# Reordering TensorE's sums in the closing normalisation of a graph-attention layer

## What is computed

```python
Q, K, V = x @ Wq, x @ Wk, x @ Wv
score = exp(clip(einsum(K[src], Q[dst]) * scale, -5, 5))
h_attn = segment_sum(V[src] * score, dst) / (segment_sum(score, dst) + 1e-6)
h = x + h_attn
mean = h.mean(axis=0); var = ((h - mean) ** 2).mean(axis=0)
y = (h - mean) * rsqrt(var + 1e-5) * bn_gamma + bn_beta      # over the nodes
z = x + y
out = (z - z.mean(-1)) / sqrt(z.var(-1) + 1e-5)              # over the features
```

## Time and profile before

| | us |
|---|---|
| median of 3 timed runs | 2000.03 (1999.54 to 2001.93) |
| the profiled execution's own time | 1993.93 |
| its span, first to last instruction | 1992.2 |
| stage A, VectorE's first instruction of `normalise` to its first subtraction | 1840.6 to 1889.7 |
| stage B, to VectorE's first `times_amp` | 1889.7 to 1927.4 |
| stage C, to the end | 1927.4 to 1992.2 |

### The profile page before, as it was taken

How to read it: one execution, slowest core, us unless ns; L and a number is a source line. 1 busy time by engine, 2 the same in 40 slices (tenths; PEclk the granted TensorE clock), 3 DMA queues, 4 the chain that set the end, 5 groups by cost and what they waited for, 6 DMA issues and landing times. The chain is left out here.

```text
span 1992.2 us, 42376 instructions
## 1 busy us (share of the span) xinstructions
PE 1905.1 (96%) x7908; PEld 1348.2 (68%) x8018; DVE 1725.7 (87%) x2477; ACT 1365.2 (69%) x4578; POOL 1362.4 (68%) x1698
## 2 busy tenths in 40 slices
PE   8999999996899999999999999999999999998788
PEld 4555555554677777777777777777777777776233
DVE  6679555555899999999999999999999999999788
ACT  0000000003899999999999999999999998998657
POOL 0103343345788888888888888888888887885776
PEclk9999999997999999999999999999999999999989
DMA  5537766768999999999999999999999999999307
GB/s 188 170 128 228 242 222 226 242 230 286 332 333 331 340 350 350 333 338 349 348 347 338 336 347 348 350 336 338 344 350 344 340 345 336 339 356 346 110 17 289
DMA packets 184221, 588.87 MB, mean 296 GB/s; under 512 B 28432, under 2 KB 30192, under 8 KB 184176
## 3 DMA queue, kind: packets, MB, share of 16 engines
q0 software_dynamic: 135904, 465.14, 64.6%
q1 hardware_dynamic: 44752, 121.39, 17.6%
q10 hardware_dynamic: 3520, 1.81, 0.3%
HBM read 535.01 MB, written 78.91 MB: 308 GB/s over the span
## 5 line engine op out<-in xcount | busy, mean ns | idle before, releaser
L656 POOL DMA_INDIRECT kv<-kv_d,idx x880 | 909.3, 1033 | 235.6 <-issue 207.5
L742 ACT ACTIVATE kv<-kv 128x64 f32<-128x64 f32 x3520 | 889.3, 335 | 14.3
L830 PE MATMUL acc<-kv,mm_sb 128*128 128x260 f32 x3520 | 844.0, 383 | 6.2 <-ACT kv L742 0.6
L830 PEld LDWEIGHTS acc<-kv,mm_sb 128*128 128x128 f32 x3520 | 667.8, 190 | 104.3 <-issue 1.0
L809 PE MATMUL q_ps<-q_tile,mm_sb 128*128 x1760 | 539.9, 429 | 29.5 <-issue 7.2
L694 DVE TENSOR_TENSOR kv<-q_ps,kv 128x1024 f32<-128x1024 f32 x440 | 537.9, 1222 | 28.8 <-issue 14.6
L701 DVE TENSOR_REDUCE raw<-kv 128x16 f32<-128x1024 f32 x440 | 532.2, 1210 | 0.0
L809 PEld LDWEIGHTS q_ps<-q_tile,mm_sb 128*128 128x128 f32 x1760 | 316.7, 189 | 167.6 <-issue 124.3
L616 DVE TENSOR_TENSOR kv<-kv 128x384 f32<-128x384 f32 x440 | 249.9, 568 | 16.7 <-ACT kv L756 16.6
L752 ACT ACTIVATE mm_sb<-mm_ps,less 128x1024 fp32r<-128x1024 f32 x220 | 241.1, 1096 | 18.0 <-issue 8.8
L362 ACT COPY p<-places 128x768 f32<-128x768 f32 x24 | 19.2, 799 | 277.6 <-PE places L299 277.6
(11 more groups left out here) (160 smaller groups left out, 1399.1 us busy)
## 6 DMA issues: line engine op xcount, KB each, us to landing
q_tile<-q_d SPq DMA_DIRECT2D x49, 512.0 KB, 7.1
kv<-kv_d,idx POOLq DMA_INDIRECT x880, 5.9
q_d<-q_a SPq DMA_DIRECT2D x25, 512.0 KB, 3.2
kv_d<-kv_a SPq DMA_DIRECT2D x25, 512.0 KB, 4.8
xb<-in_x POOLq DMA_DIRECT2D x49, 256.0 KB, 3.9
xb_d<-xb POOLq DMA_DIRECT2D x49, 256.0 KB, 2.8
out_rows<-agg SPq DMA_DIRECT2D x49, 256.0 KB, 2.1
x_sb<-in_xT SPq DMA_DIRECT2D x24, 512.0 KB, 6.9
```

Source lines behind the costliest of these rows:

```text
L656: pool.indirect_dma_start(kv[:, s, u, 0:2 * DIM], None, kv_d, bass.IndirectOffsetOnAxis(idx[:, s, u:u + 1], 0), bounds_check=N_NODES - 1, ...
L742: return act.activation(v, v, ACT.Copy, scale=kv[:, s, u, 2 * DIM + h:2 * DIM + h + 1])
L830: last = pe.matmul(acc[:, bass.ds(par, 1), DIM - (1 - n) * HALF:DIM + n * HALF], m, kv[:, sc, u, DIM + n * HALF:DIM + (n + 1) * HALF], sta ...
```

## The change

Three edits in `normalise`.

```diff
-FIVE, POOL_PLACES = 5, 42
+FIVE, POOL_PLACES = 5, 40
...
-        AFTER = 3
+        AFTER = 7
...
                 lines = [t for t in range(TILES) if on_pe(t)]
-                add_x(lines[0])
+                for t in lines[:Y_BANKS]:
+                    add_x(t)
                 for n, t in enumerate(lines):
-                    if n + 1 < len(lines):
-                        add_x(lines[n + 1])
+                    if Y_BANKS <= n + 2 < len(lines):
+                        add_x(lines[n + 2])
                     pe.wait_ge(s_y, n + 1)
                     pe.matmul(line(t), ident[:, :], row(t), start=False, stop=True).then_inc(s_yx, 1)
```

## The result

The changed kernel takes 2006.55 us (median of 10 runs, 2003.43 to 2009.89) against 2001.79 us before (10 runs, 1999.54 to 2005.89). The ratio is 1.0023, with a 95% interval of 1.0013 to 1.0033: 4.8 us slower by the medians, where +5.7 was forecast. The median before is now over ten runs; over the first three, on which the forecast of 2005.7 us was built, it was 2000.03, so part of the nearness of 2006.55 to 2005.7 is the 1.8 us by which that start moved.

A forecast was written before the change was run, and what follows sets the result against it. VectorE was taken to bound `normalise`, but for two waits on TensorE. The terms -4.55 - 2.85 + 12.4 + 0.7 = +5.7 us, added to the median of 2000.03, gave 2005.7 us, range 2001.5 to 2009.5.

The forecast's parts named there:

- Stage A: Sums seven places behind and place 41 on VectorE let the subtractions in `normalise` start 4.55 us earlier.
- Stage B: VectorE's 49 subtractions in `normalise` keep their instructions and length: 0, with 0.3 us to either side.
- Seven additions ahead: At stage C's start, seven additions of x fill TensorE's idle time and keep its clock full: -2.85 us.
- The distance: In stage C, adding x of line n+2 ahead of tile n stalls seven moments by 1.77 us each: +12.4 us.
- The new idle stretch: TensorE idles 2.75 us before tile 8 in stage C; a clock fall costs 1.4 us, about even chance: 0.7.
- that the stalls don't come: Rival: stage C's seven stalls are absent, leaving -7.4 us, 1992.6 us; chance 0.08.
- only 0.7 to 1.2 us long: Rival: stage C's stalls are shorter because normalisation comes earlier relative to VectorE; -2 to +2 us, chance 0.06.
- that stage A gives nothing: Rival: something other than place 41 and the pairs holds stage A's sums; +10 us, 2010, chance 0.04.
- That the clock falls within the groups: Rival: TensorE's clock falls at each of stage C's seven stalls, +12 us on top, 2017; chance 0.06.

The follow-up runs named there:

- Place 41 alone: Kernel before with only the addition of place 41 moved from GpSimd to VectorE, pairs still summed three places behind: stage A 46.99 us, timed once.
- nine places: Kernel with everything of the change but the longer distance, pairs summed nine places behind instead of seven: ratio 0.9967 to the kernel before.
- n+3: Changed kernel with x of line n+3 instead of n+2 added ahead of tile n: stage C 103.55 us, timed once.

## Why the prediction was right, step by step

- **Stage A, -4.55 us:** measured -4.50, and 4.52 in the kernel with nothing else changed. Place 41 alone brings 2.08 of it. The eleven sums from pair 33 on, without a gap, stand in the trace. The size holds for executions whose clock stays in stage A before; against the mean of the four old ones the gain is 5.0.
- **Stage B, 0:** 37.70 and 37.71 us. In one kernel, that with stage A's edits alone, the clock was at half for 6.8 us in it and not for 3.4, and it took 38.51, which is more than the 0.3 us that the prediction allowed.
- **Seven additions ahead, -2.85 us:** -2.88 against the profile on which the sum was made. The mechanism is right (the fill keeps the clock at full, and without a fall there is nothing to give back), but the size holds only for that execution. Over the five executions with the old order the mean is 63.46 us, so on average the fill brings 1.5 us and not 2.85. This is the term that was mis-sized for a median over many runs.
- **The distance, +12.4 us:** 74.38 to 61.93 us in stage C, with the fill in both: 12.45. Seven waits, at the places that were named, 1.77 us late each by starts (3.11 less 1.34). The bounds of 1.5 to 3.5 were kept. It was read from a wait of the trace of before that cost nothing there, since the tile behind it had 0.2 us to spare. The tile behind the waiting addition didn't pass it in any group. That matmuls stay in program order stands in the Trainium skill ("TensorE: Matmul & The Clock Gate", Step-by-step: what each phase is for). The seven waits of 1.7 us agree with it.
- **The new idle stretch, 0 to 1.4 us, taken as 0.7:** nothing was lost in either profile. The prediction made the stretch 2.75 us long. It was 2.57: x was added 1.11 us after the shift, close to the 1.08 reckoned, but TensorE ended tile 6 some 0.2 us later than it had said. To put 0.7 for an even chance mixed two cases into one number; the profile shows the one that gives +5.0 in the sum, and +5.05 was measured.
- **Rivals:** that the stalls don't come (-7.4) or are only 0.7 to 1.2 us long is settled by the traces, with seven stalls of 1.77; that stage A gives nothing, by its -4.50. What the -7.4 names is the kernel with all but the distance, 144.17 us against 151.59. That the clock falls within the groups did not happen with n+2 and happened with n+3.
- **The median:** +4.8 and, the second time, a ratio of 1.0030, about +6.0 us. With the means of the old order instead of the profile's values, in stage A as in stage C, the sum is -4.96 - 1.55 + 12.45 = +5.9. That lies inside both ratios' intervals (+2.6 to +6.6 and +3.8 to +8.0 us), and no finer split of the median is shown. In part it was luck that the forecast came out so near: for the mean, the fill was put 1.3 us too large and stage A's gain 0.4 too small, and the 0.7 for the idle stretch was not spent. These three nearly cancel.

## What to carry to other kernels

To work further ahead through a ring of buffers makes each user wait for a more recent release, and in an engine that works in order, what stands behind that wait waits too: look up when the release becomes due, above all where it comes in batches, and how much slack the work behind it has. A wait in the trace that costs nothing now served here to reckon what it costs one step earlier, 1.77 us to the hundredth. Filling idle banks ahead of a stage and lengthening the distance in the steady state are two changes. The second costs 12.4 us here; the first brings 1.5 us in the mean of the profiles, which the time of the kernel with it alone doesn't show clear of noise.

## What the runs showed of the hardware

The same idle time doesn't always have the same effect on TensorE's clock. After 3.90 us of idle time it was at half for 6.8 us, at half for 3.4 us, or still at full. After 2.57 us it was at full in the profile before, and at half in the second execution of the same kernel; there the lost time was 1.7 us in stage A. After 5.12 us, and after each idle stretch of 3.24 to 3.83 us with three lines ahead, it was at half. It fell behind shorter ones too, after 1.47 us in stage A with nine places; and in stage B, behind waits of 1.44 and 1.42 us, it was at half for 3.4 us in twelve of the fourteen executions, for 6.8 us in one and not at all in one, of which only the 6.8 us lengthened the stage (38.51 us against 37.71). A forecast from one profile therefore carries up to 2.9 us of luck in such a place, more than anything else in this kernel's last 150 us: stages whose clock fell alike repeat to within 0.1 us (44.53 to 44.57, 37.70 to 37.72, 61.89 to 61.94, 74.37 to 74.38), and the three of stage C with 3.4 us at half to within 0.3 (63.35 to 63.61). The Trainium skill ("TensorE: Matmul & The Clock Gate", Why this matters for your kernels) warns of idle gaps between bursts of matmuls that take the clock back to half. The traces agree in the direction, with 5.12 us and half clock behind it, and show by 1.47 us with a fall and 3.90 us without one that the length of a gap alone doesn't decide it.
